# Issuing the sums of a row block two steps behind its masks instead of one, in a four-layer graph network

## The reference

```python
deg = jnp.clip(jnp.sum(adj, axis=-1, keepdims=True), 1.0, None)
agg = jnp.einsum('bij,bjd->bid', adj, x) / deg
out = agg @ Wr + x @ Wx + b
nrm = jnp.maximum(jnp.linalg.norm(out, axis=-1, keepdims=True), NORM_EPS)
return out / nrm * mf[..., None]
```

## Time and profile before

| what | us |
|---|---|
| median of 3 runs | 1270.97 |
| lowest and highest run | 1269.97, 1272.73 |
| the profiled execution, its own time | 1272.81 |
| its span, first to last instruction | 1271.1 |
| PE busy | 1149.8 |
| DVE busy | 769.3 |
| ACT busy | 589.4 |
| mean granted TensorE clock, as a share of full speed | 0.957 |

### The profile page before, as it was taken

How to read it: one execution, slowest core, us unless ns; L and a number is a source line. 1 busy time by engine, 2 the same in 40 slices (tenths; PEclk the granted TensorE clock), 3 DMA queues, 4 the chain that set the end, 5 groups by cost and what they waited for, 6 DMA issues and landing times. The chain is left out here.

```text
span 1271.1 us, 26866 instructions
## 1 busy us (share of the span) xinstructions
PE 1149.8 (90%) x9713; PEld 930.8 (73%) x9713; DVE 769.3 (61%) x2819; ACT 589.4 (46%) x1533; POOL 114.6 (9%) x129
## 2 busy tenths in 40 slices
PE   4999889986798988989899999899998899996998
PEld 4999766754587777777699999699998555543554
DVE  5998587766556676666534545444545546546983
ACT  3888566777454455445303343413334433323441
POOL 3343000000000000000000000031323011010000
PEclk9999888875899999999999999999999999998999
DMA  8967011210465556662326664146666336633921
GB/s 329 336 266 276 24 31 28 36 19 15 167 265 201 191 207 250 248 233 117 130 110 259 254 244 183 51 166 229 269 238 243 133 133 265 250 147 146 406 61 50
DMA packets 105513, 228.92 MB, mean 180 GB/s; under 512 B 34528, under 2 KB 53152, under 8 KB 105376
## 3 DMA queue, kind: packets, MB, share of 16 engines
q1 hardware_dynamic: 104656, 227.07, 48.1%
q10 hardware_dynamic: 720, 0.07, 0.0%
HBM read 185.70 MB, written 37.75 MB: 176 GB/s over the span
## 5 line engine op out<-in xcount | busy, mean ns | idle before, releaser
L1459 PE MATMUL lay_acc<-lay_z,k_otheradj 128*128 128x128 f32 x1024 | 118.1, 277 | 0.0
L1459 PE MATMUL lay_acc<-lay_z,k_keepadj 128*128 128x128 f32 x1024 | 117.0, 275 | 0.0
L1459 PEld LDWEIGHTS lay_acc<-lay_z,k_otheradj 128*128 128x128 f32 x1024 | 116.9, 194 | 0.0
L1459 PEld LDWEIGHTS lay_acc<-lay_z,k_keepadj 128*128 128x128 f32 x1024 | 115.6, 192 | 0.0
L1507 ACT ACTIVATE lay_junk<-lay_o 128x128 bf16<-128x128 f32 x128 | 37.7, 296 | 125.2 <-DVEq L1596 125.0
L1573 DVE TENSOR_TENSOR lay_o<-lay_ring,k_vec 128x512 f32<-128x512 f32 x32 | 22.1, 692 | 108.2 <-PE lay_ring L1452 108.2
L1553 POOL TENSOR_TENSOR lay_bl<-k_vec,k_mask 128x256 f32<-128x256 f32 x32 | 21.2, 662 | 606.3 <-DVEq L1586 602.6
L333 PE MATMUL att_acc<-att_rhs,att_adjT 128*128 128x130 f32 x512 | 59.8, 280 | 13.5 <-POOLq L285 12.3
L333 PEld LDWEIGHTS att_acc<-att_rhs,att_adjT 128*128 128x128 f32 x512 | 59.2, 196 | 14.0 <-POOLq L285 12.4
L1190 ACT ACTIVATE fuse_dist<-fuse_prank,k_kb 128x512 f16<-128x512 f32 (+2 forms) x64 | 38.4, 599 | 60.7 <-PE fuse_prank L1080 59.3
L1141 PE MATMUL fuse_acc<-fuse_z,k_otheradj 128*128 128x129 f32 x512 | 63.6, 277 | 0.9 <-DVEq L1291 0.8
(11 more groups left out here) (294 smaller groups left out, 2563.0 us busy)
## 6 DMA issues: line engine op xcount, KB each, us to landing
k_keepadj<-in_adj_cols SPq DMA_DIRECT2D x28, 1024.0 KB, 9.2
k_keepadj<-keptT SPq DMA_DIRECT2D x12, 2048.0 KB, 10.8
k_otheradj<-keptT SPq DMA_DIRECT2D x12, 2048.0 KB, 10.9
att_adjT<-in_adj_cols SPq DMA_DIRECT2D x16, 1024.0 KB, 7.8
k_otheradj<-in_adj_cols SPq DMA_DIRECT2D x16, 1024.0 KB, 10.2
keptT<-k_keepadj SPq DMA_DIRECT2D x16, 1024.0 KB, 5.1
keptT<-k_otheradj SPq DMA_DIRECT2D x16, 1024.0 KB, 4.9
lay_rowf<-in_adj_rows SPq DMA_DIRECT2D x32, 512.0 KB, 14.6
```

The lines of the kernel that those rows point to most:

```text
L1459: mm = t.matmul(acc[i % 2][k][:, ib % HB, :], adjT[i % 2][:, jb, ib * P:(ib + 1) * P], zz[i % 2][:, jb, :], start=(jb == 0), stop=(jb == N ...
```

## The change

The sums of row block `jb` are issued in step `jb + 2` instead of step `jb + 1`. In step 1 there are then none. Behind the last step the blocks 6 and 7 follow, where only block 7 did. The line in `if b < B and st > 1` guards the first two steps. Nothing changes in number, shape, operands or waits of any instruction, and the lists of the other engines stay as they are.

```diff
                         for use in misc_uses(b, st):
                             side_work(*use)
-                        if b < B and st > 0:
-                            sums(b, st - 1)
+                        if b < B and st > 1:
+                            sums(b, st - 2)
                     if b < B:
+                        sums(b, NB - 2)
                         sums(b, NB - 1)
```

## The result

The changed kernel takes 1284.30 us (median of four runs, 1283.88 to 1284.59) against 1271.62 us for the kernel before in the same comparison (four runs, 1269.97 to 1272.73). The ratio is 1.010, with a 95% interval of 1.0083 to 1.0118. It is slower by 12.7 us. The forecast was 1285.2 us with a range of 1282.0 to 1290.5. One execution of the run `filled` further down (1973.55 us) and one of the kernel before beside it (1378.80 us) stand far outside the others of the same kernels, and the ratios leave them out.

A forecast was written before the change was run, and what follows sets the result against it. PE was taken as 90% busy, but held by DVE before step 2's masks. Losses of 12.53 (graph ends), 0.91 (graph 0) and 0.8 us (clock) make 14.24; added to 1270.97 they give 1285.2 us, range 1282.0 to 1290.5.

The forecast's parts named there:

- The release of the masks of step 2 doesn't depend on the sums of block 0: Step 1, graphs 1 to 7: DVE's first product starts the masks, still 7.25 us after graph start; moving sums gains nothing.
- A block costs 1.79 us at the end of graphs 1 to 7: Step 7: three blocks of sums stand together instead of two; loss 1.79 us per graph, 12.53 us over seven.
- Steps 2 to 6 give nothing back: Each step keeps one block of sums; starts and PE's waits, 2.49 us per graph from DVE and ACT, stay.
- Graph 0: No outputs ahead of it: 0.88 us gained from earlier masks, 1.79 paid at the end, net loss 0.91 us.
- Loads: DMA loads for the graph after next: chunks 2 and 3 come up to 1.8 us later, at no cost.
- The clock: A 3.1 us stop lowers PE's clock in most of graphs 1 to 7, absorbed in 1 to 6; 0.8 us, bounds 0 to 12.0.
- The sum: Eight graphs: 12.53 + 0.91 us, plus 0.8 for the clock, gives 14.24 us slower.
- The reason given for the hole: Step 1: DVE normalises the previous graph's sums (outputs, 2.79 us) before step 1's products, so PE waits before step 2's masks.
- The rival of a dearer clock: The slower clock isn't absorbed in the graphs: 15.5 to 25.4 us slower, 1286.5 to 1296.4 us; chance 0.15.
- the rival in which each graph recovers what graph 0 does: DVE's step 1 products move up, masks start earlier: loss only 0.91 us per graph, 7.3 in all, 1278.3 us; chance 0.06.

The follow-up runs named there:

- filled: The changed kernel with step 1's projection matmuls issued three times in graphs 1 to 7; 1284.37 to 1288.58 us, ratio 1.0116 to the kernel before.
- three_behind: The changed kernel with sums issued three steps behind their masks, four blocks at the graph's end; 1297.74 us, ratio 1.0215 to the kernel before.
- first_kept: The changed kernel with row block 0's sums back in step 1, so step 2 holds none; 1286.50 us, ratio 1.0108 to the kernel before.
- mean_early: The kernel before, with the next graph's row means on DVE moved from step 2 to step 7 of the graph before; 1257.97 us, ratio 0.9901.
- mean_dist: mean_early with ACT's rectification of the previous graph's result moved behind step 2's distances; 1252.06 us, ratio 0.9837 to the kernel before.
- late_moved: The kernel before, with only row block 5's sums moved from step 6 to step 7; 1274.00 us against 1274.43, ratio 1.0003.
- mean_filled: mean_early with sums two steps behind and step 1's projection issued three times in graphs 1 to 7; 1275.15 us, ratio 1.0023 to the kernel before.
- no_finish_two: mean_early with sums two steps behind, and graphs 0 to 6 without DVE's outputs and weights and ACT's squares and rectification; 1249.03 us.

## Why the prediction was right

- *The release of the masks of step 2 doesn't depend on the sums of block 0.* Right, to the hundredth: 7.25 us after the graph's start in graph 2 of both kernels and of `filled`. In graph 7 it is 6.99 and 6.98.
- *A block costs 1.79 us at the end of graphs 1 to 7.* Right: 1.78 to 1.82 in graphs 1 to 6, twice that in `three_behind`.
- *Steps 2 to 6 give nothing back.* Right. `first_kept` shows it for another step, `mean_early` and `mean_dist` show what holds them, and `late_moved` shows that it has ended by step 6, from which a block can be taken without loss.
- *Graph 0: 0.91 us.* Measured 0.89. DVE's add ends at 339.01 and its products follow at 339.13. The ranks of step 5 start 17.26 us behind the graph's start (350.80 - 333.54) for 18.15 before, so 0.89 us was won by then, against 1.79 paid at the end.
- *Loads: nothing.* Right: no product waited for a transfer, and the lengths are accounted for without one.
- *The clock: falls in most of graphs 1 to 7, absorbed in 1 to 6; 0.8 us in the sum.* The fall came in all seven and was absorbed in six. The reason given for it holds, but its sizes don't. The prediction weighed 1.72 us of lateness against 2.49 us of waits. In graphs 3 and 5 the windows lack 3.4 us, about 3.0 and 2.9 of it behind the stop by my estimate, so by these figures some 0.4 to 0.5 us should have shown, and none did (39.36 and 39.37 us). The waits in brackets understate what is to spare, as the 1.52 us for 0.82 in `mean_filled` show. Two terms were too small and made up for each other, which is luck. In graph 7 the fall cost 3.41 - 1.79 = 1.62 us, against up to 1.4 weighted with 0.6. So the term measured 1.6 in this execution, for 0.8. By the rule of the Trainium skill, "TensorE: Matmul & The Clock Gate", section "HAM oscillation — how this bites in real kernels", as the prediction applies it, the whole half-rate loss would have become wall time. In this loop 1.6 us of it did, of five falls of 1.7 us and two of 3.4.
- *The sum.* The eight graphs lost 15.06 us for 14.24 predicted. The medians differ by 12.7; the 2.4 us between are in the phases that the change doesn't touch. The 2.27 us won ahead of the graphs in the profiled pair lie well inside the 6.3 us by which the same instructions vary there (last section); for the part behind them no run settles it. Inside the phase the forecast was 0.8 us too low, and against the medians 1.5 too high.
- *The reason given for the hole* was `outputs`. It is a part of it: `no_finish_two` still lost 1.51 of 1.79. This didn't change the number, since the trace's release time carried it.

The rival of a dearer clock and the rival in which each graph recovers what graph 0 does are both out, by `filled` and by the 7.25 us. What the first named for itself, a fall that lasts two stretches, did happen in graphs 3 and 5, and cost nothing.

## What to carry to other kernels

Ask of a piece of work that is to be issued later whether the engine waits right behind its old place for something that doesn't depend on it; if so, the piece is free where it is and costs its full length wherever the engine is the late one. More distance between producer and consumer helps only if the consumer waited on that producer: here the sums never waited for their own masks' product. The idle time in brackets is less than what an engine has to spare; the start times of the same work in a trace without the wait give the whole (5.48 us for 7.00). The waits themselves were worth attacking on the engine that was late: moving 2.3 us of DVE work into its pause and one block of ACT work behind a more urgent one gave 1.6%.

## What was unexpected of the hardware

The granted clock falls at a stop of 3.1 us in every one of seven graphs, and with 1.8 us of repeated matmuls in the hole (stop 1.32) in none of graphs 1 to 6. In graph 7 of `filled` it fell nevertheless, behind a stop of 1.27 us, and it did so again in `mean_filled` (0.95 there, 1.00 in its graphs 1 to 6). The windows of `filled`:

```profile
612.00:614.00 2.00, 0.93 (x9) 0.73 (x7) 1.55 (x5) 1.80 (x13) 0.00 (x0) 1.00 0.01 4
614.00:616.00 2.00, 1.46 (x13) 0.98 (x14) 1.63 (x4) 0.77 (x5) 0.00 (x0) 1.00 0.08 31
616.00:618.00 2.00, 2.00 (x11) 2.00 (x12) 1.57 (x8) 1.43 (x5) 0.00 (x0) 0.55 1.02 410
```

The length of the stop alone doesn't tell, and it didn't in the kernel before either. The prediction names a stop of 2.16 us behind which the clock stayed at 1.00, but the same trace has two of 2.15 us, before 816.05 and 1000.64, with a granted clock of 0.50 over 816 to 818 us and 0.54 over 1000 to 1002. Nor does it set how long the clock stays low: behind the same stop of 3.10 us, graphs 2 and 3 of the changed kernel lacked 1.7 and 3.4 us of full-rate time. What decides these cases no run here shows.

The phases ahead of the changed one move by themselves: the first mask stood between 332.5 us (`mean_early`) and 338.8 us (`first_kept`) in twelve executions of the same instructions up to that point, one for each kernel. That is more than the sums of three row blocks. A change of under 0.3% is read from the lengths inside its phase, not from the medians.
